# A graph-attention layer with gate and layer norm: v by DRAM and broadcasting DMAs, the adjacency in PSUM

## The reference

```python
h = einsum('bnd,ade->bane', x, W);  th = tanh(h)
attn = th @ w_src + (th @ w_dst).T          # per head, 512 x 512
attn = where(attn >= 0, attn, 0.2 * attn);  attn = where(adj, attn, -999)
feat = elu(softmax(attn) @ h + b)           # heads side by side
gate = sigmoid(x @ H_w.T + H_b)
out = layernorm(x + gate * feat + (1 - gate) * x)
```

## Time and profile before

| | us |
|---|---|
| median of 3 runs (736.37 to 737.73) | 736.47 |
| the profiled execution, its own time | 738.14 |
| its span, first to last instruction | 736.3 |
| busy: PE / DVE / POOL / ACT | 694.9 / 688.7 / 586.6 / 382.0 |
| mean granted clock of TensorE, of its full speed | 0.985 |
| DMA: moved, mean rate | 43.82 MB, 60 GB/s |

### The profile page before, as it was taken

The page is one execution under the profiler, slowest core; times in us unless marked ns, Lnnn a source line. Parts: engine busy times, 40 slices in busy tenths (PEclk is TensorE's granted clock), DMA queues, the critical chain, the costliest instruction groups (busy, mean ns, idle before and its releaser), DMA issues.

```text
span 736.3 us, 12754 instructions
## 1 busy us (share of the span) xinstructions
PE 694.9 (94%) x3473; PEld 398.2 (54%) x3530; DVE 688.7 (94%) x1283; ACT 382.0 (52%) x807; POOL 586.6 (80%) x434
## 2 busy tenths in 40 slices
PE   8899999999999999999999999999999999999970
PEld 5555556555555655555555555555656555563530
DVE  7899999999999999999999999999999999999876
ACT  5423456373655637365563736556373655636161
POOL 2865897979989797998979799897989989793500
PEclk9999999999999999999999999999999999999995
DMA  5020213111131211113121121213111131111102
GB/s 186 28 74 1 57 44 101 44 44 57 45 100 43 100 43 43 57 43 100 43 100 43 43 57 43 100 43 100 43 43 57 43 100 43 58 44 43 44 1 85
DMA packets 32875, 43.82 MB, mean 60 GB/s; under 512 B 1234, under 2 KB 26580, under 8 KB 32852
## 3 DMA queue, kind: packets, MB, share of 16 engines
q1 hardware_dynamic: 24660, 31.35, 13.8%
q10 hardware_dynamic: 8192, 12.19, 4.6%
HBM read 30.95 MB, written 12.58 MB: 59 GB/s over the span
## 4 chain that ended last, share of the span: by engine, by line
PE 77%; DVE 14%; issue 4%; ACT 2%; DMA 1%; DVEq 0%; POOL 0%; ACTq 0%; SPq 0%; POOLq 0%
PE out_T L879 40%; PE hg L792 26%; DVE ew L638 8%; PE tr L887 4%; PE vb L863 4%; PE hg L848 1%; DVE sd L587 1%; DVE ex L673 1%; ACT h_sb L405 1%; DMA xT_in<-in_xT 1%; DVE att L656 1%; PE hg L853 1%; DVE ex L735 1%; DVE th_w L572 0%; DMA out<-y 0%
## 5 line engine op out<-in xcount | busy, mean ns | idle before, releaser
L638 DVE SCALAR_TENSOR_TENSOR ew<-vb,u,adj_in 128x512 f32<-128x512 f32 x768 | 533.3, 738 | 1.8 <-PE vb L863 1.8
L879 PE MATMUL out_T<-ew,vals 128*64 128x512 f32 x1536 | 361.1, 600 | 2.8 <-DVE ew L638 1.3
L879 PEld LDWEIGHTS out_T<-ew,vals 128*64 128x64 f32 x1536 | 110.3, 136 | 195.2 <-issue 161.9
L274 POOL TENSOR_TENSOR th_w<-th,score_w 128x768 f32<-128x768 f32 x58 | 107.4, 1852 | 64.7 <-ACT th L401 54.5
L434 ACT ACTIVATE att_T<-out_T,tiny 128x512 f32<-128x512 f32 x96 | 66.2, 689 | 140.6 <-PE out_T L879 140.4
L792 PE MATMUL hg<-w_hi,xT_hi 128*128 128x384 f32 x384 | 108.5, 391 | 10.0 <-ACT h_sb L405 6.6
L792 PE MATMUL hg<-w_lo,xT_hi 128*128 128x384 f32 x384 | 88.4, 338 | 0.0
L792 PE MATMUL hg<-w_hi,xT_lo 128*128 128x384 f32 x384 | 88.0, 337 | 0.0
L278 POOL TENSOR_TENSOR th_w<-th_w 128x384 f32<-128x384 f32 x58 | 78.1, 1346 | 4.5
L411 ACT ACTIVATE gate_tanh<-hg 128x384 f32<-128x384 f32 x64 | 31.4, 491 | 96.0 <-PE hg L792 96.0
L792 PEld LDWEIGHTS hg<-w_hi,xT_hi 128*128 128x128 f32 x384 | 69.7, 192 | 19.3 <-issue 15.3
(11 more groups left out here) (107 smaller groups left out, 791.6 us busy)
## 6 DMA issues: line engine op xcount, KB each, us to landing
xT_in<-in_xT SPq DMA_DIRECT2D x16, 768.0 KB, 4.7
x_in<-in_x SPq DMA_DIRECT2D x16, 768.0 KB, 4.5
out<-y ACTq DMA_DIRECT2D x15, 768.0 KB, 3.5
adj_in<-in_adjT SPq DMA_DIRECT2D x16, 256.0 KB, 4.9
ew<-in_W SPq DMA_DIRECT2D x1, 576.0 KB, 4.3
scratch<-in_HwT SPq DMA_DIRECT2D x1, 576.0 KB, 8.0
score_w<-in_w_rows SPq DMA_DIRECT2D x1, 384.0 KB, 7.2
out<-y SPq DMA_DIRECT2D x1, 384.0 KB, 2.5
```

The source lines that it names most:

```text
L274: g.tensor_tensor(th_w[:, c % 2], th[:, c].unsqueeze(1).broadcast_to([P, 2, D]), score_w[:], ALU.mult).then_inc(S["thw_done"], 1)
L638: ve.scalar_tensor_tensor(out=ew[:, (2 * C * j + i) % SLOTS, :], in0=VB[h % 4][:], scalar=u[:, q, c, h:h + 1], in1=adj_in[:, q, c, :], op0 ...
L879: te.matmul(OUT[VW * k:VW * k + VW, :], vals[:, q, c, h, :], ew[:, t % SLOTS, :], start=(c == 0), stop=(c == C - 1)).then_inc(S["ew_free"], 1)
```

## The change

v stays in float32 and is not split: ACT writes it once, PE transposes it by four float32 transposes, now right behind `attend` 3 rather than 4, ACT copies the [12, 512] result to SBUF behind `copy_out` 3, and SP stores it to a DRAM scratch, waits for that store, and loads it again pair by pair (`load_v`), each load with a source of 4 KB that is repeated for all 128 partitions, into three slots of `v_all`. The 192 products of `broadcast_v`, `split_v` and the selecting matrices are gone. The four PSUM banks that this frees hold the adjacency as float32, one bank a chunk; ACT converts it (`adjacency`), once a batch, between `row_squares` and `copy_out` 5. The tile instruction of DVE now reads v from SBUF and the adjacency from PSUM. The adjacency bytes have one buffer in place of two, `scratch` two slots in place of four. The setup of POOL is shorter by the selecting matrices, `mean_w` is one column that is broadcast, and the warm-up products are fewer and of zeros.

```diff
-        adj_in = sb("adj_in", [P, 2, C, N], U8)
+        adj_in = sb("adj_in", [P, C, N], U8)
...
-        v_parts = sb("v_parts", [P, C, P], BF16)
-        v_T = sb("v_T", [P, 2, N], BF16)
+        v = sb("v", [P, C, H])
+        zeros = sb("zeros", [P, P], BF16)
+        v_T = sb("v_T", [H, N])
+        v_all = sb("v_all", [P, VSLOTS, 2, N])
...
-        scratch = sb("scratch", [P, C, D])
+        scratch = sb("scratch", [P, 2, D])
...
-        VB = [pb("vb0"), pb("vb1"), pb("vb2"), pb("vb3")]
+        ADJ = [pb("adj0"), pb("adj1"), pb("adj2"), pb("adj3")]
...
+        NSC = 4
+        NEX = 4
...
+        v_rows = nc.dram_tensor("v_rows", [2, H, N], F32, kind="Internal").ap()
...
+                store_v(0, 0)
+                sp.wait_ge(S["st_v"], 16)
+                for j in range(VSLOTS):
+                    load_v(0, 0, j)
+
+            def store_v(b, q):
+                sp.wait_ge(S["vT_done"], b + 1)
+                sp.dma_start(v_rows[q], v_T[:]).then_inc(S["st_v"], 16)
+
+            def load_v(b, q, j):
+                rows = v_rows[q, 2 * j:2 * j + 2, :].rearrange("(o k) n -> o k n", o=1)
+                sp.dma_start(v_all[:, j % VSLOTS], rows.broadcast_to([P, 2, N])).then_inc(ld_v[j % VSLOTS], 16)
...
-                if not first and not last:
-
-                    sp.wait_ge(S["alone_done"], b + 1)
+                if not last:
+
+                    sp.wait_ge(S["adj_done"], C * b + C)
                 if ahead:
                     load_xT(b + 2)
                 if not last:
-                    sp.dma_start(adj_in[:, 1 - q], adj_v[b + 1]).then_inc(ld_adj[1 - q], 16)
+                    sp.dma_start(adj_in[:], adj_v[b + 1]).then_inc(S["ld_adj"], 16)
+                for j in range(VSLOTS, HP):
+                    sp.wait_ge(S["ew_ready"], 4 * H * b + 2 * C * (j - 2))
+                    load_v(b, q, j)
                 if not first:
                     sp.wait_ge(S["x_forms_done"], b)
                     sp.wait_ge(S["mixed"], 3 * b + 3)
                 sp.dma_start(x_in[:], x_v[b]).then_inc(S["ld_x"], 16)
+                if not last:
+                    store_v(b + 1, 1 - q)
+                    sp.wait_ge(S["st_v"], 16 * b + 32)
+                    for j in range(VSLOTS):
+                        if j:
+                            sp.wait_ge(S["ew_ready"], 4 * H * b + 2 * C * (j + 4))
+                        load_v(b + 1, 1 - q, j)
...
-                act.wait_ge(S["pool_setup"], SETUP)
-                a.activation(head_sel[:], row_sel[:].unsqueeze(2).broadcast_to([P, H, P]), ACT.Copy).then_inc(S["head_sel_done"], 1)
+                for c in range(C):
+                    adjacency(0, c)
...
-                a.activation(v_parts[:, :, 0:H], s_pos[:], ACT.Exp, scale=ALPHA - 1).then_inc(S["exps_done"], 1)
-                a.activation(v, s_pos[:], ACT.Exp, scale=ALPHA - 1).then_inc(S["exps_done"], 1)
+                a.activation(v[:], s_pos[:], ACT.Exp, scale=ALPHA - 1).then_inc(S["exps_done"], 1)
             def copy_vT(b, q):
                 act.wait_ge(S["vtp_done"], b + 1)
-                a.activation(v_T[:, q], vtp, ACT.Copy).then_inc(S["vT_done"], 1)
+                act.wait_ge(S["st_v"], 16 * b)
+                a.activation(v_T[:], vtp, ACT.Copy).then_inc(S["vT_done"], 1)
+
+            def adjacency(b, c):
+                act.wait_ge(S["ld_adj"], 16 * b + 16)
+                if not isinstance(b, int) or b:
+                    act.wait_ge(S["ew_ready"], 4 * H * b - 2 * C + 2 * c + 2)
+                a.activation(ADJ[c][:], adj_in[:, c], ACT.Copy).then_inc(S["adj_done"], 1)
...
+                    if c > 1:
+                        act.wait_ge(S["sums_done"], C * b + c - 1)
+                    a.activation(scratch[:, c % 2], y[:, c], ACT.Copy, accum_out=sums[:, c:c + 1]).then_inc(S["sums_done"], 1)
...
                     exps(b + 1, 1 - q)
                 copy_out(b, 3)
+                if not last:
+                    copy_vT(b + 1, 1 - q)
                 gates(b, 3)
                 if not first:
                     row_sums(b - 1)
...
                     for c in range(C):
                         split(b + 2, q, c)
                 copy_out(b, 4)
-                if not last:
-                    copy_vT(b + 1, 1 - q)
                 if not first:
                     row_squares(b - 1)
+                if not last:
+                    for c in range(C):
+                        adjacency(b + 1, c)
                 copy_out(b, 5)
...
-                for f in scores_rel(0) + split_v(0):
+                for f in scores_rel(0):
...
-            def split_v(b):
-
-
-                def rest():
-                    dve.wait_ge(S["exps_done"], NEX * b + NEX)
-                    ve.tensor_tensor(v_rest, v, v_parts[:, :, 0:H], ALU.subtract).then_inc(S["scores"], 1)
-
-                def middle():
-                    sc(b, 5)
-                    ve.tensor_copy(v_parts[:, :, H:2 * H], v_rest).then_inc(S["scores"], 1)
-
-                def low():
-                    sc(b, 6)
-                    ve.tensor_tensor(v_parts[:, :, 2 * H:3 * H], v_rest, v_parts[:, :, H:2 * H],
-                                     ALU.subtract).then_inc(S["scores"], 1)
-
-                return [rest, middle, low]
-
...
-                    if c == 0:
-                        dve.wait_ge(S["vb_ready"], H * b + h + 1)
+                    if j == 0 and k == 0:
+                        dve.wait_ge(S["adj_done"], C * b + c + 1)
+                    if i == 0:
+                        dve.wait_ge(ld_v[j % VSLOTS], 16 * (2 * b + j // VSLOTS + 1))
                     dve.wait_ge(S["ew_free"], 4 * H * b + 2 * C * j + i + 1)
-                    ve.scalar_tensor_tensor(out=ew[:, (2 * C * j + i) % SLOTS, :], in0=VB[h % 4][:], scalar=u[:, q, c, h:h + 1],
-                                            in1=adj_in[:, q, c, :], op0=ALU.max, op1=ALU.mult).then_inc(S["ew_ready"], 1)
+                    ve.scalar_tensor_tensor(out=ew[:, (2 * C * j + i) % SLOTS, :], in0=v_all[:, j % VSLOTS, k], scalar=u[:, q, c, h:h + 1],
+                                            in1=ADJ[c][:], op0=ALU.max, op1=ALU.mult).then_inc(S["ew_ready"], 1)
...
-                    if j == 4 and not last:
-                        between |= {i: [f] for i, f in zip((1, 2, 3), split_v(b + 1))}
...
                 max_T(0)
-                warm_up(4, ident_bf[:], ident_bf[:])
+                warm_up(1)
                 max_all(0)
-                warm_up(2 * WARM, ident_bf[:], ident_bf[:])
+                warm_up(WARM // 2)
                 transpose_v(0)
-                pe.wait_ge(S["head_sel_done"], 1)
-                warm_up(2, ident_bf[:], head_sel[:, 0:4].rearrange("p h n -> p (h n)"))
-                broadcast_v(0, 0, 0)
-                broadcast_v(0, 0, 1)
-
-            def warm_up(n, l, r):
+                warm_up(WARM)
+
+            def warm_up(n):
                 for _ in range(n):
-                    te.matmul(TR[:, 0:r.shape[1]], l, r, start=True, stop=True)
...
             def transpose_v(b):
-                pe.wait_ge(S["scores"], NSC * b + NSC)
-                for c in range(C):
-                    last = te.transpose(vtp[:, c * P:(c + 1) * P], v_parts[:, c], ident_bf[:])
+                pe.wait_ge(S["exps_done"], NEX * b + NEX)
+                for c in range(C):
+                    last = te.transpose(vtp[:, c * P:(c + 1) * P], v[:, c], ident[:])
                 last.then_inc(S["vtp_done"], 1)
-
-            def broadcast_v(b, q, h):
-
-                if h == 0:
-                    pe.wait_ge(S["vT_done"], b + 1)
-
-                if h > 3 or not isinstance(b, int) or b:
-                    pe.wait_ge(S["ew_ready"], 4 * H * b + 2 * C * (h // 2 - 2) + 2 * C - 1 + h % 2)
-                te.matmul(VB[h % 4][:], head_sel[:, h], v_T[:, q], start=True, stop=True).then_inc(S["vb_ready"], 1)
...
-                broadcast_v(b, q, 10)
+                if not last:
+                    transpose_v(b + 1)
                 gates(b, q, 3, last)
                 transpose_out(b, 3)
-                broadcast_v(b, q, 11)
                 attend(b, q, 4)
-                if not last:
-                    transpose_v(b + 1)
                 means(b, q)
                 transpose_out(b, 4)
-                if not last:
-                    broadcast_v(b + 1, 1 - q, 0)
-                    broadcast_v(b + 1, 1 - q, 1)
                 attend(b, q, 5)
```

More of the change, by code:

```diff
@@ L38, in gat_layernorm @@
     SLOTS = 16
-    SETUP = 19
+    SETUP = 13
     DVE_SETUP = 12
     WARM = 12
-    NPART = 3
+    VSLOTS = 3
     assert N == 512 and H * E == D and B % 2 == 0
@@ L70, in gat_layernorm @@
         ident = sb("ident", [P, P])
-        ident_bf = sb("ident_bf", [P, P], BF16)
-        row_sel = sb("row_sel", [P, H], BF16)
-        head_sel = sb("head_sel", [P, H, P], BF16)
         low_row = sb("low_row", [P, 1])
-        mean_w = sb("mean_w", [P, P])
+        mean_w = sb("mean_w", [P, 1])
         half = sb("half", [P, C])
```

(52 more changed lines are left out.)

38 lines of the change are left out of this document (11 added, 27 removed).

## The result

The changed kernel takes 749.37 us, median of 4 runs (748.43 to 751.16), against 736.55 (736.37 to 737.73) for the kernel before: 12.8 us more, a ratio of 1.0175 with a 95% interval of 1.0156 to 1.0194. The prediction was 745.3 and slower, in a range of 731 to 763. The profiled execution is the slowest of the four, 751.16; its span is 749.4 and its mean granted clock 0.979. A step's length, from first tile to first tile, is taken from the starts of all 768 tiles.

The account below looks back on a forecast made before the run. DVE was taken to pace the kernel, PE close behind; after the change, bank 0's chain sets the step. Start 6.2, step 0 -0.8, steps +4.9, end -1.5 sum to +8.8 us: median 745.3, range 731 to 763.

Parts of the forecast that it names:

- steps 1 to 5 of the chain: Within a step: DVE to second head_sums, POOL's row to the mean, ACT's squares, adjacency bank 0, DVE's first tile at 43.4 us.
- The size of the step's loss: Steps 1 to 14: each 0.35 us longer than before because of the wait for adjacency bank 0, +4.9 us in all.
- Step 5 of the chain: From the end of ACT's bank 0 conversion to DVE's first tile: DVE sees it 0.1 us later, at 43.4.
- its step 1: DVE from a step's first tile to the end of the second head_sums: 16.66 us, after removing waits of 0.30 and 0.07.
- rival C: DVE's tile slows 18% if its SBUF operand meets POOL; step 46.2 us, total 794; chance 0.04.
- DVE's wait before the tile: At a step's first tile, DVE waits 2.5 us for adjacency bank 0, being 2.5 us faster for itself.
- waits before `rden`: DVE's waits for PE's transposes, part of some 1.85 us a step, expected to be next to none after the change.
- 40.87 for DVE's own work: DVE's step if nothing new waited: 43.08 less 0.36 for split_v and 1.85 of waits for PE, 40.87 us.
- A: Bank 0 is there in time and DVE bounds the step at 40.87 us; total 709; chance 0.14.
- B: The first tile waits for v's store and load through DRAM, 1.3 us a step; total 763; chance 0.10.
- D: TensorE's clock falls to 1.2 GHz for part of each step and PE takes the lead; about 770; chance 0.04.
- The start: Before the first tile: conversions, v's transposes, copy, store and load put it at 30.4 us, +6.2 us, bounds +3.1 and +6.6.

Follow-up runs that it names:

- experiment 1: Changed kernel with ACT converting adjacency banks 0 and 1 ahead of the squares; 734.12 us, ratio 0.9966.
- experiment 2: Changed kernel with adjacency bank 0 converted twice, one extra conversion between the squares and bank 0; 756.29 us, ratio 1.0268.
- experiment 9: Changed kernel with the gates' third product term (x_lo by w_hi) left out, 12 PE products a step less; 744.21 us, ratio 1.0101.
- experiment 4: Changed kernel with the adjacency read as bytes from SBUF, no conversions, squares' scrap in PSUM, so the tile reads two SBUF operands; 1114.75 us.
- experiment 6: Against experiment 1: PE transposes output pair 2 before the maximum's product and pair 3 before v, ACT copies v after gates 3; 732.26 us.
- experiment 8: Experiment 1 with the gates' third product term (x_lo by w_hi) also left out, 12 PE products a step less; 723.46 us, ratio 0.9813.
- experiment 5: Changed kernel with every batch storing v once more to another DRAM scratch and waiting for it before any load; 750.59 us, ratio 1.0185.

## Why the prediction was right, and where it was off

**The mechanism.** The steps 1 to 5 of the chain hold. Measured from the first tile, predicted and in the profile after: end of the second `head_sums` 16.66 and 16.79; `weigh` 3 at 16.80 and 16.94; POOL's row 23.43 and 23.44; squares ended 42.78 and 42.92; first bank 43.30 and 43.40; first tile 43.4 and 43.65. Experiment 1 shows it by taking the chain off (15.3 us less), experiment 2 by lengthening it, experiment 9 by taking work off PE, which left the step within 0.15.

**The size of the step's loss** was the term that failed: 0.35 predicted (43.4 less 43.08 is in fact 0.32), 0.59 measured, 3.4 of the 4.1 us by which the forecast was low. Two parts of it can be read off. Step 5 of the chain took 0.1 us from the conversion's end to the tile; it is 0.25 (377.35 to 377.60). And the end of its step 1 is 0.13 later. It took `elu` from before, 2.08 us; it now takes 2.36 in this step, 0.28 more, of which the rest of that stretch, a little shorter than counted, gives 0.15 back. The cause is that of experiment 4: `elu` reads two SBUF operands. In the step above POOL's L290 ran from 347.00 to 348.01; `elu` started at 347.27, when that had 0.74 left, and took 0.60 more than its undisturbed 1.76. In the kernel before, POOL's operation of that moment had 0.46 left, and `elu` took 0.32 more. The same holds in the other profiled kernels: `elu` takes 1.62 us and what POOL's operation has left when it starts (2.23 for 0.61 in experiment 9, 2.45 for 0.83 in the next step of the changed kernel). I had named this stretching for the tile, as rival C, and not asked what it does to the one instruction of the chain that was known to have it, once it meets POOL at another moment.

**DVE's wait before the tile** was predicted at 2.5 and was 1.0, because the waits before `rden` did not go. I had counted 192 products less on PE, named DVE as the engine that paces the kernel, and taken the waits for gone. A view of before that the prediction does not use speaks against it: part 4 of the page, the chain of work that ended last, lay on PE for 77% of the span, and with the bank out of the way it lies there for 89% (kernel before, then experiment 1):

```profile
PE 77%; DVE 14%; issue 4%; ACT 2%; DMA 1%; DVEq 0%; POOL 0%; ACTq 0%; SPq 0%; POOLq 0%
PE 89%; DVE 3%; ACT 3%; DMA 2%; issue 2%; POOL 0%; SPq 0%; ACTq 0%; POOLq 0%; DVEq 0%
```

The wait at j = 3 fell only from 1.37 to 0.87, and one of 0.60 came at j = 4 where none had been. Part of what PE was spared it now spends waiting itself, for DVE's tiles (the weight loads of `attend`, kernel before, then after; in experiment 1, where no tile waits for a bank, it is 55.8 us):

```profile
PEld out_T L879 <- DVE ew L638: 28.0, 89, 2.1
PEld out_T L873 <- DVE ew L647: 76.7, 170, 2.1
```

So the two engines are not in step by their totals. v's transposes now stand ahead of `gates` 3 and of the transposes that `rden` of j = 4 waits for; experiment 6, which put them behind both, took 0.33 of the 0.60 away, and experiment 8 shows that PE's load is in both waits. How much of the 0.87 is order and how much load is not shown. In the changed kernel these waits cost nothing in the steps: experiment 9 took most of them away and got the time back as a wait for the bank, 2.06 us long. Where the chain is off the path they are what counts. That this wrong term did not move the forecast is luck: the bank sets the step whatever DVE waits for before it, up to the 2.5 us. The step of 42.58 in experiment 1 less its 1.46 is 41.12, that of 41.92 in experiment 8 less 0.79 is 41.13, and 43.65 of the changed kernel less 0.98, 0.87 and 0.60 is 41.20. So the 40.87 for DVE's own work was low by 0.25 to 0.33. `elu`, over its 2.08, is 0.28 of that in the changed kernel and 0.21 in experiment 8, but 0.07 in experiment 1; and the 1.85 us of waits that were taken off came out too high, since the trace before has DVE idle for 1.70 us a step.

**The rivals.** A (709, no wait for the bank): the bank does set the step, and with it out of the way the time is 734, not 709; the rival's price was wrong, for the waits before `rden` stay. B (v late): v had 4.5 us to spare in the step shown, where 3.4 had been counted, and experiment 5 used 1.6 of it for nothing. C (the tile slows): 734 ns; it is what happens when the second operand is in SBUF too. D: the mean granted clock of the four runs was 0.979 to 0.987 against 0.985 in the profile of before, and PEclk is at 9 in every slice but the last. In the profiled execution the clock was at 1.2 GHz for 3.4 us from 7.5, from 31.4 and from 686.7, and from 727.7 on: nowhere in steps 1 to 14.

**The start.** +6.2 predicted and +6.21 in the profile, but with errors that cancel: the copy of v ended at 23.38 (23.6 predicted), the store took 1.5 us from issue to the next issue and not 2.3, and from the load's issue at 24.93 to the first tile it was 5.5 and not 4.5. These are the rows:

```profile
22.79 0.59 ACT L438 ACTIVATE v_T<-hg 12x512 f32<-12x512 f32 x1 [0.69 <-PE hg L856]
23.41 0.32 SPq L198 DMA_DIRECT2D v_rows<-v_T  x1
24.93 2.01 SPq L202 DMA_DIRECT2D v_all<-v_rows  x3
30.41 6.01 DVE L647 SCALAR_TENSOR_TENSOR ew<-v_all,u,adj 128x512 f32<-128x512 f32 x9 [9.44 <-DMA v_all<-v_rows]
```

In the other profiled kernels the last stretch took 4.1 to 5.4 us, and why the first load is mostly slower than the 3.7 of the median one stays open. The start moves by itself, too: v's copy began anywhere between 21.2 and 22.8 in kernels whose start is the same, so a term of the start is known to about 1 us from one profile. The Trainium skill, page "DMA: Bandwidth & Descriptors", section "Anatomy of one DMA", has the fixed 2.0 us and the rate for DMAs that GpSimd issues, which the prediction did not say; these are issued by SP. Carried over to them all the same, it gives 2.1 us for the store and 3.2 for the load, as an estimate; at the start the store was quicker (1.5), and the load slower (3.7 in the median of all). By this estimate the start would have cost 4.9; the trace has 6.21.

**Step 0 and the end.** Step 0 gave 0.73 for 0.8. The last step gave 0.75 for 1.5: the products left out there gave half of what I had put down for them.

## What to carry to other kernels

When an engine near its bound is relieved, find the next wait before counting the gain, and then look at the order in which the releasing engine does its work: here ACT's conversion stood behind squares that stood behind a mean, and moving two of four conversions ahead of them was worth 15 us, more than the 12.8 that the change had cost. Less work on a releasing engine need not shorten the waits for it by as much: 12 products a step fewer here took DVE's waits for PE from 1.64 us a step to 1.46, and 12 others, in the gates, from there to 0.73. Read the chain that ended last before saying which of two busy engines sets the pace. And ask of an operand that is moved from PSUM to SBUF whether the other one stands there too: beside a busy POOL that cost 1114.75 us against 749.37 here.

## What the runs showed of the hardware that was not expected

- A DVE instruction with two SBUF operands and a POOL instruction wait for each other whole: tiles of 0.73 us took 3.5 and 3.9 us beside POOL's operations of 3.89 and 3.75 (experiment 4), and `elu` of 1.76 took 2.36 when a POOL instruction of 1.01 had started 0.27 before it. The other way round, POOL's L278 of 1.02 took 2.40 in the kernel before when it started 0.54 after `elu`.
- It makes next to no difference which operand of the tile is in PSUM: 738 ns with v there, 734 ns with the adjacency there.
- From the end of ACT's write to PSUM to the start of the DVE instruction that waits for it: 0.25 us (0.22 on average of steps 1 to 14); a conversion of 128 x 512 bytes to float32 in PSUM takes 0.58 alone and 2.14 for four.
- A store of 24 KB to DRAM, waited for, costs 1.5 us at the start, and 2.6 in a step, where x's load of 768 KB stands ahead of it; a load of 512 KB, in which two rows are read by all 128 partitions, costs 3.7 us in the median (3.3 to 6.9), six of them a step beside 2.5 MB of other transfers without anyone waiting.
